# Projecting the queries' latent side in four terms instead of six, with the parts added across partitions by VectorE

## The reference

```python
q = rmsnorm(x @ q_a_w.T, q_a_ln) @ q_b_w.T          # 16 heads x (64 nope + 64 rope)
ckv = x @ kv_a_w.T                                  # 32 latents + 64 rope, shared by the heads
kv = rmsnorm(c, kv_a_ln) @ kv_b_w.T                 # per head 64 nope + 128 values
query = concat(q_nope, rope(q_pe)); key = concat(k_nope, rope(k_pe))
scores = einsum('bhsd,bhtd->bhst', query, key) * scale
attn = softmax(scores); out = einsum('bhst,bhtd->bhsd', attn, v)
return out.transpose(0, 2, 1, 3).reshape(B, S, H * VD) @ o_w.T
```

## Time and profile before

| | |
|---|---|
| median of 3 runs | 1949.65 us (1948.52 to 1953.75) |
| the profiled execution's own time | 1951.45 us |
| its span in the trace | 1949.6 us |
| mean granted TensorE clock | 0.976 |
| TensorE busy | 1851.4 us (95%) |
| VectorE busy | 1254.6 us (64%) |
| ScalarE busy | 1384.7 us (71%) |
| GpSimd busy | 1383.7 us (71%) |

### The profile page before, as it was taken

How to read it: one execution, slowest core, us unless ns; L and a number is a source line. 1 busy time by engine, 2 the same in 40 slices (tenths; PEclk the granted TensorE clock), 3 DMA queues, 4 the chain that set the end, 5 groups by cost and what they waited for, 6 DMA issues and landing times. The chain is left out here.

```text
span 1949.6 us, 43870 instructions
## 1 busy us (share of the span) xinstructions
PE 1851.4 (95%) x13730; PEld 981.7 (50%) x13730; DVE 1254.6 (64%) x2826; ACT 1384.7 (71%) x1908; POOL 1383.7 (71%) x837
## 2 busy tenths in 40 slices
PE   8979999999999999999999999999889689999986
PEld 6734444444444444444444444444376467777765
DVE  5777777767776777677767776776076345555553
ACT  5617888888888888888888888888752145555543
POOL 1526888988898889888988898889747723333330
PEclk9969999999999999999999999999999889999998
DMA  6100122112111211121112211000024379999979
GB/s 251 49 10 1 65 98 89 66 63 112 74 66 63 110 76 66 63 110 76 66 63 108 78 66 52 8 6 10 7 86 184 135 247 345 338 350 354 346 270 302
DMA packets 104645, 240.00 MB, mean 123 GB/s; under 512 B 24656, under 2 KB 57680, under 8 KB 104464
## 3 DMA queue, kind: packets, MB, share of 16 engines
q1 hardware_dynamic: 93840, 209.18, 30.2%
q0 software_dynamic: 10752, 30.16, 4.0%
HBM read 130.66 MB, written 104.37 MB: 121 GB/s over the span
## 5 line engine op out<-in xcount | busy, mean ns | idle before, releaser
L899 POOL TENSOR_TENSOR prob_lo<-prob,prob_hi 128x1024 f16<-128x1024 f32 x512 | 1080.8, 2129 | 166.4 <-ACT prob_hi L928 166.4
L974 DVE TENSOR_REDUCE maxes<-ring 128x1 f32<-128x512 f32 x1024 | 645.2, 684 | 232.4 <-PE ring L1065 229.9
L926 ACT ACTIVATE prob<-p_s,prob_scale 128x1024 f32<-128x1024 f32 x512 | 571.1, 1115 | 212.2 <-PE p_s L1084 190.7
L928 ACT ACTIVATE prob_hi<-p_s,prob_scale 128x1024 f16<-128x1024 f32 x512 | 570.3, 1114 | 0.0
L1065 PE MATMUL ring<-kr_hi,qr_hi 64*128 64x512 f16 x1024 | 374.8, 384 | 7.7 <-DVE qc_hi L961 4.2
L1065 PE MATMUL ring<-kc_pair,qc_hi 64*128 64x512 f16 x1024 | 371.3, 383 | 0.0
L1084 PE MATMUL p_s<-qr_lo,kr_hi 64*128 64x512 f16 x1024 | 287.0, 375 | 0.0
L1084 PE MATMUL p_s<-qr_hi,kr_lo 64*128 64x512 f16 x1024 | 286.5, 376 | 0.0
L1353 POOL DMA_INDIRECT ranked_out<-y,dest x128 | 123.1, 962 | 216.2 <-DVE y L1660 213.5
L1084 PE MATMUL p_s<-qr_hi,kr_hi 64*128 64x512 f16 x1024 | 244.2, 380 | 1.6 <-ACT prob_hi L928 1.6
L1084 PE MATMUL p_s<-qc_lo,kc_one 33*128 33x512 f16 x1024 | 242.4, 378 | 0.0
(11 more groups left out here) (248 smaller groups left out, 2447.4 us busy)
## 6 DMA issues: line engine op xcount, KB each, us to landing
w<-in_experts SPq DMA_DIRECT2D x128, 608.0 KB, 5.3
expert_rows<-zeros SPq DMA_DIRECT2D x129, 544.0 KB, 4.7
rows<-expert_rows SPq DMA_DIRECT2D x128, 136.0 KB, 4.7
got<-ranked_out SPq DMA_DIRECT2D x16, 768.0 KB, 10.4
wqb<-in_wqb SPq DMA_DIRECT2D x8, 768.0 KB, 4.9
recip_wide<-prob_recips SPq DMA_DIRECT2D x64, 64.0 KB
cbar<-att_t SPq DMA_DIRECT2D x64, 64.0 KB, 2.0
cbar<-in_woT SPq DMA_DIRECT2D x1, 2048.0 KB, 16.8
```

The source lines that it names most:

```text
L899: gp.tensor_tensor(prob_lo[s % NB][:, :], prob[s % 2][:, :], prob_hi[s % NB][:, :], ALU.subtract).then_inc(lo_ready, 1)
L926: act.activation(prob[s % 2][:, :], p_s[s % 2][:, :], ACT.Exp, bias=prob_scale[:, :], scale=SCALE / W_SCALE)
L928: act.activation(prob_hi[s % NB][:, :], p_s[s % 2][:, :], ACT.Exp, bias=prob_scale[:, :], scale=SCALE / W_SCALE).then_inc(p_ready, 1)
L974: best = v.tensor_reduce(maxes[:, at:at + 1], bank[:, :], AX.X, ALU.max)
```

## The change

The latent side (side 1) is projected with the high and the low weights side by side as one stationary operand. Columns 0 to 31 hold the high weights and 32 to 63 the low ones; this meets the high part of h. A second operand with the high weights and 32 zero columns meets the low part of h. So four matmuls per c stand where six stood. The bank's rows 0 to 31 then hold the high weights' products and rows 32 to 63 the low weights' product, and the same for the other c in rows 64 to 127. VectorE copies each block of 32 rows to its partner's rows of `rot` and adds `rot` to the bank, which gives the full sum in both blocks. The copies and the add stand in `split` between `qr_hi` and `qc_hi`. ScalarE lays `wq` out with one copy more per head, and GpSimd clears the 32 zero columns once at the start, ahead of its other clears, so that the counts of `zero_rows` and `wq_ready` grow by one.

```diff
-STEPS_V = 2 * 8 + 2
+STEPS_V = 2 * 8 + 12
...
-            sp.wait_ge(zero_rows, 3)
+            sp.wait_ge(zero_rows, 4)
...
+            blank = wq[:, :].rearrange("p (k n) -> p k n", k=2 * DK)[:, DK:2 * DK, ROPE + C:P]
+            gp.memset(blank, 0.0).then_inc(zero_rows, 1)
+            gp.wait_ge(zero_rows, 1)
             gp.memset(prob_scale[:, :], float(np.log(P_SCALE))).then_inc(zero_rows, 1)
...
                 act.copy(wide[:, :, 0:ROPE], w3[:, :, ds(h * KA, ROPE)]).then_inc(wq_ready, 1)
-                for n in range(2):
-                    act.copy(wide[:, :, ROPE + n * C:ROPE + (n + 1) * C],
-                             w3[:, :, ds(h * KA + ROPE, C)]).then_inc(wq_ready, 1)
+                for to, at, from_ in ((0, ROPE, 0), (0, ROPE + C, DK), (DK, ROPE, 0)):
+                    act.copy(wide[:, to:to + DK, at:at + C], w3[:, from_:from_ + DK, ds(h * KA + ROPE, C)]).then_inc(wq_ready, 1)
...
                 v.wait_ge(ring_mm, use + 1)
+                for dst, src in ((0, C), (C, 0), (ROPE, ROPE + C), (ROPE + C, ROPE)):
+                    step.mark(v.tensor_copy(rot[dst:dst + C, :], bank[src:src + C, :]))
+                step.settle()
+                step(v.tensor_tensor(bank[:, :], bank[:, :], rot[:, :], ALU.add))
                 v.tensor_copy(qc_hi[half][:, :], bank[:, :]).then_inc(q_ready, 1)
...
-                terms = [(k, w, t) for k in range(DK) for w, t in ((0, 0), (0, 1), (1, 0))]
+                terms = [(k, w, t) for k in range(DK) for w, t in (((0, 0), (0, 1), (1, 0)) if side == 0 else ((0, 0), (1, 1)))]
...
-                pe.wait_ge(wq_ready, 3 * h + 3)
+                pe.wait_ge(wq_ready, 4 * h + 4)
```

More of the change, by code:

```diff
@@ L877, in _ @@
         def _(gp):
+            blank = wq[:, :].rearrange("p (k n) -> p k n", k=2 * DK)[:, DK:2 * DK, ROPE + C:P]
+            gp.memset(blank, 0.0).then_inc(zero_rows, 1)
+            gp.wait_ge(zero_rows, 1)
             gp.memset(prob_scale[:, :], float(np.log(P_SCALE))).then_inc(zero_rows, 1)
-            gp.wait_ge(zero_rows, 1)
+            gp.wait_ge(zero_rows, 2)
             gp.memset(maxneg[:, :], 0.0).then_inc(zero_rows, 1)
-            gp.wait_ge(zero_rows, 2)
+            gp.wait_ge(zero_rows, 3)
             gp.memset(zeros[:, :], 0.0).then_inc(zero_rows, 1)
             for n in range(2):
-                gp.wait_ge(zero_rows, 3 + n)
+                gp.wait_ge(zero_rows, 4 + n)
                 gp.memset(recip_wide[n][:, :], 0.0).then_inc(zero_rows, 1)
@@ L1018, in _ @@
             half_head(0, 0, first=True)
-            v.wait_ge(zero_rows, 5)
+            v.wait_ge(zero_rows, 6)
             half_head(0, 1)
@@ L1118, in half_head @@
                         weigh(kt, m)
-            pe.wait_ge(zero_rows, 2)
+            pe.wait_ge(zero_rows, 3)
             project_rope(0, 0, 0, ring[0])
```

## The result

The changed kernel takes 1993.59 us (median of 4 runs, 1989.93 to 2003.66) against 1951.24 before (4 runs, 1948.52 to 1953.75): ratio 1.0241, 95% interval 1.0218 to 1.0264 (the two medians alone give 1.0217). It is slower, as forecast, but by 42 us and not by 25, and outside the range. The profiled execution has a span of 1992.0 us, 42.4 more than before.

The account below looks back on a forecast made before the run. TensorE, busy 95% of the span, was taken as the bound, with VectorE's slack only before copy_out. Half-heads 16.5, prologue 7.4, ScalarE 0.2 and clock 1 sum to 25.1 us on 1949.65: about 1975 us, range 1969 to 1980.

Parts of the forecast that it names:

- the shift of 3.72: VectorE's chain in split: four copies and one add delay qc_hi and everything after it by 3.72 us.
- The rival with a step of 0.60: Copies in split step at 0.60, not 0.72; the half-head grows by 0.07 us, 1959 us in all; chance 0.10.
- The prologue: Before half-head 0: no cover, so two TensorE waits each grow by VectorE's 3.72 us, +7.4 us.
- ScalarE's 0.2: Before the first matmul: ScalarE's one extra copy, which that matmul waits for, costs at most +0.2 us.
- the clock: Before half-head 0: a 5.6 us wait may lower TensorE's clock, costing 0 to 3 us, taken as +1.
- Where it lands: Half-head start: copy_out moves from 665.23 to 665.77, the fourth maximum from 666.57 to 667.12; 30 x 0.55 = +16.5 us.
- the 39.56 that I had: Steady part: forecast length in us of the changed kernel's half-head, which took 39.01 before.
- My third rival: TensorE's stall costs more than its length, by clock or restart; 1984 us with a restart of 0.2 to 0.4; chance 0.11.
- The sign that I gave for it: Profile after: a half-head longer than 39.7 us with copies at 0.72 means the stall has its own price.
- 0.44 us of TensorE per half-head: Latent side's matmuls: two of six pairs go, at 0.22 us each.
- VectorE's slack holds it: Rival for split: slack covers the five instructions, TensorE's saving stays; 5 to 9 us faster, 1943 us; chance 0.04.
- the 1.0 us that I put at the fourth maximum: Next half-head's fourth maximum: TensorE stands about 1.0 us, waiting for VectorE's first reduce.

Follow-up runs that it names:

- e10: e5 with its four copies of 32 x 512 all from partitions 0 to 31 to partitions 0 to 31 of a separate tile; ratio 1.0059.
- e6: The changed kernel with two copies of 64 x 512 that don't change partitions in place of the four of 32 x 512; ratio 1.0024.
- e5: The changed kernel, loop kept, with the wait for qc_lo's ring_used and the step of q_ready moved behind copy_out; ratio 1.0139.
- e9: e5 without the copies and the add in the prologue's two splits; ratio 1.0107.
- e2: The changed kernel without the four copies and the add; ratio 0.9988.
- e8: e2 with GpSimd's subtraction cut to half its columns for key tiles 14 and 15; ratio 0.9949.
- e1: The changed kernel with VectorE's loop over heads 1 to 14 written out; ratio 1.0152.
- e7: The changed kernel with VectorE's loop written out, q_ready's step behind copy_out, and six maxima in group 4, four in group 5; ratio 1.0121.

## Why the prediction was wrong

**What held.** The place and the mechanism: VectorE's chain in `split`, `copy_out`, first reduce, fourth maximum. The copy at 0.72 with the row L490 as its price (2.84 us for four, exact), the add at 0.74, the shift of 3.72. The Trainium skill's rule in "VectorE: DVE Perf Modes", "Two Vector instructions with no wait between them", is borne out by e10 (same partitions, 0.59) and e6 (the first copy, which starts where `qr_hi` did, follows at 0.61). The rival with a step of 0.60 is refuted for copies that change their place. The clock stayed at 1.00 in the half-heads and fell before half-head 0. The prologue was sized at 8.4 us (without ScalarE's 0.2). From the kernel before to e5 it costs 9.0, 7.5 for the two chains and about 1.5 for the clock, where I had 1; against e9 it is 9.4. One reading of the rule was loose without changing anything: the first copy changes only its input's partitions, not its output's; it is held all the same, at 0.72 behind `qr_hi`.

**The step that failed** is in "Where it lands": "it starts at 661.45 + 3.72 + 0.60 = 665.77". I took the step of 0.60 between `qc_lo` and `copy_out` from rows in which no wait for VectorE's own result stands between the two instructions. In the program there are, in this order, a wait for `qc_lo`'s own `ring_used`, the step of `q_ready`, the branch of the loop (every second time) and two waits with computed values. Before, they stood under a 3.1 us wait, where none of my rows showed them. I used up that cover and gave its content no price. It is 1.01 - 0.60 = 0.41 and 1.42 - 0.60 = 0.82 us in turn, 0.615 on average: 29 x 0.615 = 17.8 us in stretch B, and the excess over 29 x 0.55 = 16.0 is 17.8 too. With the one wait moved (e5) the half-head is 39.57 against the 39.56 that I had, and stretches A and B with the last two half-heads are 25.3 us longer than before, where the sum without ScalarE's term is 24.9. The ratio of the whole is 1.0139, 27 us.

My third rival, a stall that costs more than its length, had the direction right and the cause wrong. Its restart of 0.2 to 0.4 us stood on no row, and neither the clock nor the restart of TensorE adds anything (0.06 us from the reduce's end to the maximum, as before). The sign that I gave for it, a half-head longer than 39.7 with the copies at 0.72, came true, and would have led me to it wrongly: the gap is on VectorE.

**A second step was wrong without showing in the result:** "0.44 us of TensorE per half-head" as a gain when VectorE has slack. It is 0.12 us (e2), since GpSimd's subtraction in group 7 takes 0.30 (e8). So the rival "VectorE's slack holds it" could have given at most 3.6 us and not 12 in the steady part (its own sum gives 4.9 us in all; the 9 and the 1943 don't follow from it). For the same reason the 1.0 us that I put at the fourth maximum is 0.32 in e5. I had read GpSimd's 34.88 of 39.01 us as over 4 us to spare in every place, the same mistake as with VectorE's 11 us.

**What the change is worth.** 0.12 us per half-head against 9.4 us in the prologue. e2, which leaves the addition out everywhere, is 4.1 us shorter than the kernel before over A, B and the last two half-heads. So even a version in which VectorE's addition hid completely in the steady part would, by an estimate from these (9.4 - 4.1), stay some 5 us behind the kernel before, unless the prologue kept its six terms, which wasn't run. e6, which has the shorter chain, is 1.0024. None of the variants that add the right parts in every half-head (e1, e5, e7) beats the kernel before.

## What to carry to other kernels

An instruction put into a chain that is followed by a wait costs nothing up to that wait's length; beyond it, everything that stood under the same cover comes out too, control work included, so list what the program has between the last instruction and the wait, not only what the timeline shows. A wait for an engine's own last result, placed between two of its instructions, is best put behind the next piece of work if nobody needs it there: moving one such wait and its step took 18 us off. A saving on the engine that is busy 100% has to be followed to the next engine in the stage where it falls: here it was worth a quarter of its size.

## What the runs showed of the hardware that was not expected

- VectorE's branch back and computed wait values cost nothing when an instruction is still running in front of them (e5: step 0.60 through the loop's end), and 0.13 us (0.34 - 0.21) and 0.53 us (0.74 - 0.21) when a wait for its own result stands ahead of them.
- The Trainium skill ("VectorE: DVE Perf Modes", "The DRAIN you can't avoid") says, of a series of eight copies, that a semaphore after each costs nothing extra. Raising one costs nothing here either (`qc_hi` raises one, and `qr_lo` follows at 0.61). Waiting for the instruction in front does: the next follows at 0.73 to 0.74 where it would follow at 0.60, and the control work behind the wait comes on top. The measurement decides.
